# First attention of a transformer pair: the key-side product made in quarters, each with a score tile, instead of once a head

## The reference, cut to what matters

```python
scores = jnp.einsum('bhqd,bhkd->bhqk', Q, K) * scale
c2p = jnp.einsum('bhqd,shd->bhqs', Q, pos_key) * scale
c2p = jnp.take_along_axis(c2p, rel_pos[None, None, :, :], axis=-1)
p2c = jnp.einsum('bhkd,shd->bhks', K, pos_query) * scale
p2c = jnp.take_along_axis(p2c, p2c_pos[None, None, :, :], axis=-1)
p2c = jnp.swapaxes(p2c, -1, -2)
probs = jax.nn.softmax(scores + c2p + p2c, axis=-1)
ctx = jnp.einsum('bhqk,bhkd->bhqd', probs, V)
```

## Time and profile before

| | |
|---|---|
| device time, median of 3 runs | 2113.69 us (2112.2 to 2116.16) |
| profiled execution, its own time | 2112.18 us |
| its span, first to last instruction | 2110.4 us |
| granted TensorE clock, mean of the span | 0.931 |
| busy: PE, DVE, ACT | 82%, 70%, 70% of the span |

### The profile page before, as it was taken

How to read it: one execution, slowest core, us unless ns; L and a number is a source line. 1 busy time by engine, 2 the same in 40 slices (tenths; PEclk the granted TensorE clock), 3 DMA queues, 4 the chain that set the end, 5 groups by cost and what they waited for, 6 DMA issues and landing times. The chain is left out here.

```text
span 2110.4 us, 44034 instructions
## 1 busy us (share of the span) xinstructions
PE 1724.6 (82%) x11670; PEld 1044.7 (50%) x11670; DVE 1468.4 (70%) x3508; ACT 1466.8 (70%) x2584; POOL 79.4 (4%) x102
## 2 busy tenths in 40 slices
PE   2316999999999999983861799999999994999998
PEld 1203555555555555552540465565556552545544
DVE  2635888888888888872983788888888882423422
ACT  2304888888888888881872799999999993223222
POOL 0000000000000000000540000000000000000000
PEclk9656999999999999996985899999999997999999
DMA  2966999998899999955687777777777763100100
GB/s 71 353 217 195 271 270 276 275 269 271 271 274 277 270 271 276 272 163 153 206 299 257 200 210 213 213 213 211 212 212 213 211 180 100 35 20 22 37 5 10
DMA packets 419996, 420.89 MB, mean 199 GB/s; under 512 B 36016, under 2 KB 325320, under 8 KB 419808
## 3 DMA queue, kind: packets, MB, share of 16 engines
q1 hardware_dynamic: 419936, 420.19, 67.1%
HBM read 232.47 MB, written 187.00 MB: 199 GB/s over the span
## 5 line engine op out<-in xcount | busy, mean ns | idle before, releaser
L817 ACT ACTIVATE a_prob<-bank,a_negmax 128x512 f32<-128x512 f32 x1024 | 734.6, 717 | 51.3 <-DVE a_negmax L749 49.6
L749 DVE TENSOR_REDUCE a_negmax<-bank 128x1 f32<-128x512 f32 x1024 | 699.5, 683 | 0.2 <-issue 0.2
L631 PE MATMUL bank<-a_ident,a_prob 128*128 128x128 f32 x4096 | 644.1, 280 | 60.1 <-ACT a_probt L824 50.8
L824 ACT COPY a_probt<-bank 128x512 f32<-128x512 f32 x1024 | 616.2, 602 | 87.4 <-PE bank L631 73.7
L631 PEld LDWEIGHTS bank<-a_ident,a_prob 128*128 128x128 f32 x4096 | 449.5, 141 | 181.9 <-issue 76.5
L741 DVE TENSOR_TENSOR bank<-bank,a_band 128x128 f32<-128x128 f32 (+3 forms) x1024 | 350.2, 342 | 80.1 <-PE bank L612 68.4
L610 PE MATMUL bank<-a_stks 65*128 65x192 bf16 (+7 forms) x1024 | 323.0, 316 | 10.5 <-ACT a_prob L817 10.2
L644 PE MATMUL bank<-a_probt,a_vs 128*32 128x512 f32 x2048 | 272.4, 606 | 15.0 <-ACT a_probt L824 15.0
L610 PEld LDWEIGHTS bank<-a_stks 65*128 65x128 bf16 (+1 forms) x1024 | 100.1, 98 | 231.8 <-ACT a_prob L817 202.4
L729 DVE COPY_PREDICATED bank<-a_mask,bank 128x128 f32<-128x128 uint32 (+1 forms) x512 | 139.4, 272 | 107.2 <-PE bank L616 107.1
L612 PE MATMUL bank<-a_stks 65*128 65x320 bf16 (+5 forms) x768 | 201.1, 262 | 0.0
(11 more groups left out here) (169 smaller groups left out, 1567.9 us busy)
## 6 DMA issues: line engine op xcount, KB each, us to landing
a_band<-shear_b SPq DMA_DIRECT2D x128, 512.0 KB, 4.4
shear_a<-a_keyside SPq DMA_DIRECT2D x128, 256.0 KB, 3.4
a_sheared<-shear_a SPq DMA_DIRECT2D x128, 256.0 KB, 4.4
shear_b<-a_corr SPq DMA_DIRECT2D x128, 256.0 KB, 4.4
shear_e<-a_corr SPq DMA_DIRECT2D x128, 256.0 KB, 2.3
a_band<-shear_e SPq DMA_DIRECT2D x128, 256.0 KB, 3.4
a_stks<-stack SPq DMA_DIRECT2D x128, 192.0 KB, 4.5
a_stks<-stack SPq DMA_DIRECT2D x128, 144.0 KB, 2.9
```

What stands on the lines that cost most here:

```text
L631: last = pe.transpose(turned_bank[k][:, n * 128:(n + 1) * 128], prob[h.slot % 2][:, n, k * 128:(k + 1) * 128], ident[:, :])
L749: v.tensor_reduce(negmax[h.slot % 2][:, n:n + 1], score[:, :], AX.X, ALU.max, negate=True).then_inc(maxed, 1)
L817: nc.scalar.activation(prob[h.slot % 2][:, n, :], score[:, :], ACT.Exp, bias=negmax[h.slot % 2][:, n:n + 1]).then_inc(exped, 1)
L824: nc.scalar.copy(probt[h.slot][:, k, :], turned_bank[k][:, :]).then_inc(copied, 1)
```

## The change

The one key-side product of 512 columns and its one copy are each cut into four. Quarter k of head j+6 is made in part k of step j, right behind the third product of that part's score tile, into columns 128 to 255 of the same bank 4 (`key_quarter`). The signal that the tile is ready (`score_mm`) is now given by the quarter. VectorE copies the quarter behind `mix` (`key_quarter_out`), and the next tile's third product waits for that copy too. `key_copied` counts quarters, and SP's write of a head's key side waits for four of them: the last comes from part 3, where before the one copy came from part 1. The quarter in part 0 is the first to need the stack of head j+6. Freed of the key side, banks 5 and 6 alternate strictly, so that each group of transposes waits for a copy two earlier. The prologue's six heads keep the whole product.

```diff
 def shear_a_write(sp, h):
-    hold(sp, key_copied, h.n + 1)
+    hold(sp, key_copied, 4 * (h.n + 1))
     sp.dma_start(shear_a[h.slot % 4, :, SPAN:SPAN + T], keyside[h.slot % 2][:, :]).then_inc(a_written, 16)
...
+def turned_bank(h, k):
+    return swing[(h.slot + k) % 2] if rel else swing[k % 2]
+def corr_bank(h):
+    return swing[h.slot % 2] if rel else other
...
         if rel:
             pe.wait_ge(fixed, BASE + tile)
+            if key is not None:
+                pe.wait_ge(key_copied, BASE + 4 * key[0].n + key[1])
             a, e = fix_cols(n)
             last = pe.matmul(other[:, 0:e - a], k[:, qhi, q], k[:, khi, a:e], start=True, stop=True)
+            if key is not None:
+                last = key_quarter(pe, *key)
         last.then_inc(score_mm, 1)
...
         if rel and k == 1:
             pe.wait_ge(corr_copied, BASE + made(h.n + corr_ahead))
-        elif rel and k == 3:
-            pe.wait_ge(key_copied, BASE + made(h.n + KEY_AHEAD + 1))
+        elif rel:
+            pe.wait_ge(copied, BASE + 4 * h.n + max(k - 1, 0))
...
+def key_quarter(pe, h, k):
+    if k == 0:
+        pe.wait_ge(stk_in[h.slot], BASE + per_stk * (h.i + 1))
+        pe.wait_ge(tab_in[h.slot // GROUP], BASE + 16 * (h.i + 1))
+    return pe.matmul(key_bank[:, 128:256], tab[h.slot][:, 0:REL], stk[h.slot][:, KLO, 128 * k:128 * k + 128],
+                     start=True, stop=True)
...
-                            if rel and k == 1 and left >= KEY_AHEAD:
-                                pe.wait_ge(copied, BASE + 4 * own.n + 1)
-                                key_side(pe, Head(i, j + KEY_AHEAD))
...
+def key_quarter_out(v, h, k):
+    if k == 0:
+        v.wait_ge(a_written, BASE + 16 * (h.n - 1))
+    v.tensor_copy(keyside[h.slot % 2][:, 128 * k:128 * k + 128], key_bank[:, 128:256]).then_inc(key_copied, 1)
...
                                     mix(v, *ahead(i, j, k, score_ahead))
+                                    if left >= KEY_AHEAD:
+                                        key_quarter_out(v, Head(i, j + KEY_AHEAD), k)
...
-                                if rel and k == 1 and left >= KEY_AHEAD:
-                                    key_out(v, Head(i, j + KEY_AHEAD))
```

More of the change, by code:

```diff
@@ L375, in attention_phase @@
                 cbank = bank[7]
-                turned_bank = [bank[5], bank[6], bank[6], bank[5]] if rel else [bank[5], bank[6]] * 2
-                key_bank, corr_bank = bank[5], bank[6] if rel else bank[4]
+                swing = bank[5:7]
+                key_bank = other
                 s_const, s_pad, held_off, blank = s("const"), s("pad"), s("held_off"), s("blank")
@@ L595, in _, with score_tile @@
                         sp.wait_ge(out_written, BASE + 16 * NG)
-                    def score_tile(pe, h, n):
+                    def score_tile(pe, h, n, key=None):
                         tile, k = 4 * h.n + n, stk[h.slot]
@@ L625, in turn @@
                             pe.wait_ge(corr_copied, BASE + made(h.n + corr_ahead))
-                        elif rel and k == 3:
-                            pe.wait_ge(key_copied, BASE + made(h.n + KEY_AHEAD + 1))
+                        elif rel:
+                            pe.wait_ge(copied, BASE + 4 * h.n + max(k - 1, 0))
                         else:
-                            pe.wait_ge(copied, BASE + 4 * h.n + (k if rel else k - 1))
+                            pe.wait_ge(copied, BASE + 4 * h.n + k - 1)
                         for n in range(NT):
-                            last = pe.transpose(turned_bank[k][:, n * 128:(n + 1) * 128],
+                            last = pe.transpose(turned_bank(h, k)[:, n * 128:(n + 1) * 128],
                                                 prob[h.slot % 2][:, n, k * 128:(k + 1) * 128], ident[:, :])
@@ L657, in correction @@
                             q = slice(128 * n, 128 * n + 128)
-                            pe.matmul(corr_bank[:, q], sheared[h.slot % 4][:, q], ident[:, :], is_transpose=True, start=True, stop=False)
-                            last = pe.matmul(corr_bank[:, q], stk[h.slot][:, QLO, q], tab[h.slot][:, REL:2 * REL], start=False, stop=True)
+                            pe.matmul(corr_bank(h)[:, q], sheared[h.slot % 4][:, q], ident[:, :], is_transpose=True, start=True, stop=False)
+                            last = pe.matmul(corr_bank(h)[:, q], stk[h.slot][:, QLO, q], tab[h.slot][:, REL:2 * REL], start=False, stop=True)
                         last.then_inc(corr_mm, 1)
@@ L667, in edge @@
                             q = slice(128 * n, 128 * n + 128)
-                            last = pe.matmul(corr_bank[:, q], stk[h.slot][:, EDGE, q], edges[:, :], start=True, stop=True)
+                            last = pe.matmul(corr_bank(h)[:, q], stk[h.slot][:, EDGE, q], edges[:, :], start=True, stop=True)
                         last.then_inc(corr_mm, 1)
@@ L678, in tensor_step @@
                             if left >= (k + score_ahead) // NT:
-                                score_tile(pe, *ahead(i, j, k, score_ahead))
+                                key = (Head(i, j + KEY_AHEAD), k) if rel and left >= KEY_AHEAD else None
+                                if rel and key is None and k == 0:
+                                    pe.wait_ge(key_copied, BASE + 4 * NHEAD)
+                                score_tile(pe, *ahead(i, j, k, score_ahead), key)
                             turn(pe, own, k)
@@ L702, in _ @@
                             for j in range(KEY_AHEAD):
-                                pe.wait_ge(key_copied, BASE + j)
+                                pe.wait_ge(key_copied, BASE + 4 * j)
                                 key_side(pe, Head(0, j))
@@ L823, in copy_turned @@
                             act.wait_ge(pv_mm, BASE + 16 * (h.use(GROUP) - vslots + 1))
-                        nc.scalar.copy(probt[h.slot][:, k, :], turned_bank[k][:, :]).then_inc(copied, 1)
+                        nc.scalar.copy(probt[h.slot][:, k, :], turned_bank(h, k)[:, :]).then_inc(copied, 1)
                     def group_out(act, h):
@@ L834, in corr_out @@
                         act.wait_ge(b_written, BASE + 16 * (h.n - 1))
-                        nc.scalar.copy(corr[h.slot % 2][:, :, :], corr_bank[:, :].rearrange("p (n r) -> p n r", n=NT)).then_inc(corr_copied, 1)
+                        nc.scalar.copy(corr[h.slot % 2][:, :, :], corr_bank(h)[:, :].rearrange("p (n r) -> p n r", n=NT)).then_inc(corr_copied, 1)
                     @block.scalar
```

6 lines of the change are left out of this document (3 added, 3 removed).

## The result

The changed kernel takes **2176.98 us** (median of 4 runs, 2167.46 to 2178.59) beside 2112.94 us (4 runs, 2112.19 to 2116.16) for the kernel before: ratio 1.0291, interval [1.0259, 1.0322]. It is slower, by 64 us, where 12 were predicted (2126 beside the 2113.69 known then). The profiled execution took 2178.59 us, 66.4 more than that of before.

A forecast was written before the change was run, and what follows sets the result against it. A compute loop across engines set the 5.95 us step; afterwards the band and stack DMA loops were to bind at 6.05. 0.10 more over 122 heads gave + 12 us, hence 2126 us, range 2100 to 2148.

The forecast's parts named there:

- Compute loop: First attention, waits through VectorE, ScalarE and TensorE: 5.95 us a step before, 5.81 with quarter copies at 0.20 each.
- too dear: Rival: a quarter copy keeps VectorE for 0.29 us, not 0.20; loop 5.99, kernel + 5 us; chance 0.07.
- Stall taken away: Third transpose group's wait for the second's copy: no term of the compute loop; chance of mattering counted in the draw, 0.14.
- Band loop: SP's later key-side write delays the band read needed by the next band add: step at least 1.56 + L, 5.96.
- L: Landing time of the band read in the band loop, taken at the median 4.4 us.
- Stack loop: Part 0's quarter needs SP's stack load one step earlier; loop through two steps, 6.12 to 6.22 us a step.
- faster rival: DMA loops do not bind if band lands within 4.25 us and stack within 4.2: - 17 us, 2097; chance 0.24.

The follow-up runs named there:

- e3: Changed kernel with both the table load and the stack load issued one step earlier: 2101.53 us, 0.9942 of the kernel before.
- e10: Changed kernel with both loads one step early, key side in two 256-column halves made in parts 1 and 2: 2130.47 us, 1.0096.
- e12: Changed kernel with both loads one step early, third transpose group again waiting for the second's copy: 2102.83 us, 0.996.
- e11: Changed kernel with both loads one step early, key side in two 256-column halves made in parts 0 and 3: 2110.17 us, 0.9997.
- e1: Changed kernel with only the table load issued one step earlier: 2136.83 us, 1.0117.
- e5: Changed kernel with ten extra unread products on TensorE ahead of the part 0 quarter's table wait, one step in four: 2159.93 us, 1.022.
- e2: Changed kernel with only every head's stack load issued one step earlier: 2185.43 us, 1.0359.
- e9: Changed kernel with both loads one step early, key side in two 256-column halves made in parts 0 and 2: 2110.01 us, 0.9995.
- e7: Changed kernel with both loads one step early and SP reading the band ahead of the key side's write: 2249.45 us, 1.0644.

## Why the prediction was right in direction and wrong in size

**Compute loop: right.** The changed kernel's VectorE, same place as the earlier trace rows:

```profile
603.54 0.28 DVE L749 COPY_PREDICATED bank<-a_mask,bank 128x128 f32<-128x128 uint32 x1
603.74 0.28 DVE L784 COPY a_keyside<-bank 128x128 f32<-128x128 f32 x1
603.94 0.68 DVE L769 TENSOR_REDUCE a_negmax<-bank 128x1 f32<-128x512 f32 x1
```

The quarter's copy costs 0.20 between starts, as taken, though it lasts 0.285. Steps of the changed kernel without a wait for a DMA take 5.80 us, predicted 5.81. The rival "too dear" falls, and e3 shows this loop nearly alone: 5.80 plus 10.2 us of band waits over some 96 steps is 5.91, seen 5.90. In the Trainium skill, "VectorE: DVE Perf Modes", section on the TRN2 errata, a fixed latency is paid once for each instruction, so that many small tiles pay it many times (its heading names operands read from SBUF; these copies read a bank and write SBUF). The traces agree in kind and give its size: by the distances between starts, the 512 columns cost 4 x 0.20 = 0.80 us as four copies, 2 x 0.33 = 0.66 as two (e10) and 0.60 as one.

**Stall taken away: worth nothing, right.** e12.

**Band loop: too dear.** The step took L = 4.4, the median of before. In the changed kernel the band landed in 4.2 and the write of the key side in 2.2. Band tile first, then that write (min/median/max):

```profile
DMA to landing us min/median/max: 3.9/4.2/6.1
...
DMA to landing us min/median/max: 2.0/2.2/3.2
```

So 1.56 + 4.2 = 5.76 lies just under the compute loop. The form of the loop was right (e11 runs on it), its term L was 0.2 too large, and 2 waits of 2.3 us are all that it cost.

**Stack loop: the step that failed.** "The quarter in part 0 needs the stack of head j+6": it needs the table too, as the order rows of the change show (`waits a0_tab_in0,a0_stk_in2`). The prediction put that wait at nothing, without a reason. In one step of four the table is issued behind the stack, 0.53 later (stack 640.18, table 640.72), and is waited for in the same place. With it, and the 5.49 us from its issue to the quarter, the prediction's own formula is (7.44 + 0.53 + 5.49) / 2 = 6.73 us for each of the two steps around a table, not the 6.1 to 6.2 from which 6.05 was taken. The band adds of n = 0 around such a table show it:

```profile
585.47 0.36 DVE L761 TENSOR_TENSOR bank<-bank,a_band 128x192 f32<-128x192 f32 x1
...
591.99 0.36 DVE L761 TENSOR_TENSOR bank<-bank,a_band 128x192 f32<-128x192 f32 x1
...
598.74 0.36 DVE L761 TENSOR_TENSOR bank<-bank,a_band 128x192 f32<-128x192 f32 x1
```

13.27 us for two steps, 6.64 each; all such pairs without a drop of the clock took 13.4 in the mean, 2 x 6.70. What the prediction did say of this loop was right: the stack landed after 4.7 in the median (4.8 and 5.0 in the earlier trace rows), the write went out 1.5 us later, TensorE waited for the stack in 59 of 122 steps, and the steps that need no new table took 6.14 us in the mean. So the direction was not luck: with the table on time (e1) the stack loop costs 25 us by itself. The table and what follows it are the other 40.

**The clock: left out.** The windows of the earlier trace rows stood at 1.00 and the prediction left it there. In 15 of the 30 steps that need a new table, TensorE stood idle for 0.9 to 2.0 us and then worked at 1.2 GHz for some 3.4 us; these steps took about 8.5 us, those with a table and no drop about 7.0, so 15 x 1.5 = 23 us by this estimate. e5 shows it by itself, 17 us, with none of the 15 left. The other 15 table steps had pauses of up to 1.7 us and no drop, so the length of the pause alone does not decide; what does is open. (A sixteenth drop, at 459 us, follows another wait, of 0.9 us.)

**The sum.** Over the phase, the start of the part 0 quarter less that of the third product less the normal 0.06 gives 43 us of waiting for the table (30 waits) and 23 for the stack (59 waits). 43 + 23 + 23 for the clock + 2 for the band - 17 for the compute loop is + 74; the phase grew by 69, the kernel by 64. The predicted + 12 was taken from the stack and band loops, with the table and the clock at nothing. Steps overlap, so a wait need not cost its full length; where exactly the 5 us between 74 and 69 are is open.

These waits can't be subtracted one at a time: the loop runs through two steps, and a load that comes on time hands its slack to the other. e1 took out 43 us of table waits and 23 of clock and returned 40 (the stack's waits grew from 23 to 44 over the phase). e2 took out the stack's 23 and lost 8 (the table's grew from 43 to 60): the two steps around a table without a drop take 13.4 us in the changed kernel and 13.5 in e2, only that the first is shorter (5.8 instead of 6.3) and the second, with the longer pause, longer (7.7 instead of 7.1); with a drop they take 14.8 in both, and drops come more often. Together the two edits returned 75.

**The faster rival** named its condition rightly, loads that land in time, and was priced at 17 us by the compute loop; e3, which meets it, gains some 11 (10.5 by the medians, 12 by the ratio 0.9942). In the profiled executions the phase of e3 is 748.9 us, 7.4 less than before. Most of what is missing is the band, waited for 20 times and 10.2 us in 570 us, where it was 12 times and 5.7 us before. Halves don't mend it: they shorten the compute loop (e9 5.68) and run into the band (e9, e11; in e9 SP also waits for the correction's write, 69.7 us in 64 waits, before it can read the band) or lengthen the loop (e10).

## What to carry to other kernels

When a product moves earlier, list every semaphore that its instruction waits for, and follow each to its DMA; the one that is needed in one step of four and issued last decides. Price such a load by the loop from the event that releases its issue round to the product that needs it, and then ask whether TensorE stands idle meanwhile, because its clock may go to its half behind such a pause. Before judging a change by its time, give its new waits one more step of lead: the same cut was worth + 64 us with late loads and - 11 with early ones.

## What the runs showed of the hardware

- **A pause of one or two microseconds can be followed by half the clock.** A pause of 1.43 us that ended at 646.2 was followed by a granted clock of 0.50 from about 646.6 to 650.0, the values' product taking 1.94 us instead of 1.06. Of the 30 pauses for a table in the changed kernel, 15 (0.9 to 2.0 us) were followed by such a stretch and 15 (up to 1.7 us) were not. With useless products in these pauses (e5) none of them was.
- **Order in the queue changed a landing more than size did.** The same key-side write landed after 2.2 us ahead of the 512 KB band read and after 5.4 behind it (medians, the changed kernel and e7). In the changed kernel the 192 KB stack load, fourth in the queue, took 4.7 us, longer than the 512 KB band read, second, with 4.2. In the Trainium skill, "DMA: Bandwidth & Descriptors", the anatomy of one DMA (there one issued from GpSimd; these are SyncE's) prices a transfer by a fixed latency and its bytes; the traces show what stands ahead of it counting for more.
- **In a burst after a pause the first land faster, the last slower.** With SP's issues bunched, the key-side write's median fell from 3.4 us before to 2.2 and the band's from 4.4 to 4.2, while the correction's write rose from 4.3 to 4.6 and the stack load from 4.3 to 4.7. The lower DMA share (0.87 instead of 0.91) does not explain it: e3, at 0.96, has 2.2, 4.2, 4.6 and 4.8.
